# An adaLN feed-forward kernel whose opening is written out anew: w_up in quarters from ScalarE's queue, ternary weights rounded by an fp16 write, the clip inside the PSUM evacuation

## What is computed

```python
y  = einsum('bct,bcd->bdt', x, cond_weights[conditions])   # x: (64, 64, 512), a 64x64 matrix for each b
h  = act_quant(fwht(y, 512)) @ weight_quant(w_up).T        # w_up: (1024, 512)
h  = square(relu(h))
o  = act_quant(fwht(h, 1024)) @ weight_quant(w_down).T     # w_down: (512, 1024)
out = x + o
# act_quant: 8 bits with a scale for each token, from the token's largest magnitude
# weight_quant: scale = max(mean|w|, 1e-5); clip(round(w / scale), -1, 1) * scale
```

## Time and profile before

| | us |
|---|---|
| median of 3 timed runs | 296.42 |
| lowest and highest | 293.67, 298.29 |
| the profiled execution | 297.55 |
| its span, first to last instruction | 295.7 |
| TensorE busy | 254.3 (86%) |
| VectorE busy | 245.7 (83%) |
| ScalarE busy | 185.0 (63%) |
| POOL busy | 168.3 (57%) |

### The profile page before, as it was taken

One profiled execution on the slowest core, in us unless ns is written; L12 is line 12 of the kernel. 1 busy time (PEld: TensorE's weight loads), 2 busy tenths in 40 slices (PEclk: granted clock), 3 DMA queues, 4 the chain that ended last, 5 costly groups with the idle time before them and its releaser, 6 DMA issues.

```text
span 295.7 us, 6449 instructions
## 1 busy us (share of the span) xinstructions
PE 254.3 (86%) x1864; PEld 209.1 (71%) x1864; DVE 245.7 (83%) x346; ACT 185.0 (63%) x237; POOL 168.3 (57%) x200
## 2 busy tenths in 40 slices
PE   0277998979899899999899989998999999967863
PEld 0267888859688688888788878887887777635531
DVE  1168799999999988999999999999989898795451
ACT  1068677758577767675867576767676765924310
POOL 8034433595858686656595659574946548474400
PEclk9999899999999999999999999999999999995996
DMA  5585441235385946465664342433343434323262
GB/s 201 206 312 201 121 114 38 88 99 141 98 170 141 162 132 114 144 97 152 104 165 94 90 87 90 88 89 71 106 88 91 90 108 125 64 80 71 92 144 84
DMA packets 67049, 35.16 MB, mean 119 GB/s; under 512 B 57170, under 2 KB 57170, under 8 KB 67026
## 3 DMA queue, kind: packets, MB, share of 16 engines
q10 hardware_dynamic: 51200, 12.59, 24.3%
q1 hardware_dynamic: 15826, 22.29, 22.6%
HBM read 13.89 MB, written 8.39 MB: 75 GB/s over the span
## 4 chain that ended last, share of the span: by engine, by line
DVE 24%; PE 21%; POOL 19%; issue 18%; DMA 6%; ACT 6%; ACTq 2%; SPq 2%; POOLq 1%; DVEq 1%
PE u_ps L576 8%; POOL p_lo L373 8%; DVE g L699 5%; PE o_ps L586 5%; POOL x_half L340 4%; DMA uqT<-uq 4%; DVE u_max L713 3%; PE h_ps L561 3%; PE z_ps L543 3%; POOL u_deq L381 3%; DVE g L693 3%; DVE x_all L650 3%; DVE out_sb L732 2%; DVE z_max L674 2%; ACT uq L457 2%
## 5 line engine op out<-in xcount | busy, mean ns | idle before, releaser
L373 POOL TENSOR_TENSOR p_lo<-g,p_hi 128x1024 fp32r<-128x1024 f32 x32 | 82.8, 2608 | 59.3 <-ACT p_hi L452 51.8
L576 PE MATMUL u_ps<-had_r,p_hi 128*128 128x256 f32 x256 | 65.6, 293 | 11.8 <-ACT uq L457 11.5
L561 PE MATMUL h_ps<-zqT,w_upT 128*128 128x256 f16 x512 | 66.7, 273 | 2.5 <-ACT g L439 2.5
L693 DVE TENSOR_TENSOR g<-g 128x1024 f32<-128x1024 f32 x32 | 66.9, 2099 | 0.2 <-issue 0.2
L586 PE MATMUL o_ps<-w_downT,uqT 128*128 128x512 f16 x256 | 62.2, 387 | 5.1 <-DMA uqT<-uq 4.5
L576 PE MATMUL u_ps<-had_r,p_lo 128*128 128x256 f32 x256 | 63.9, 286 | 0.0
L576 PEld LDWEIGHTS u_ps<-had_r,p_hi 128*128 128x128 f32 x256 | 49.8, 195 | 16.5 <-issue 14.7
L340 POOL TENSOR_TENSOR x_half<-x_all 128x512 f32<-128x512 f32 (+1 forms) x32 | 43.5, 1361 | 21.2 <-DMA x_all<-in_x_dram 14.9
L561 PEld LDWEIGHTS h_ps<-zqT,w_upT 128*128 128x128 f16 x512 | 47.6, 98 | 10.4 <-issue 3.1
L439 ACT ACTIVATE g<-h_ps 128x512 f32<-128x512 f32 x64 | 36.5, 596 | 27.0 <-PE h_ps L561 13.0
L528 PE MATMUL y_ps<-w_diag,x_half 128*128 128x128 f32 (+1 forms) x256 | 38.5, 299 | 15.4 <-DMA w_diag<-in_L_cond_weights_dram 11.1
(11 more groups left out here) (42 smaller groups left out, 252.8 us busy)
## 6 DMA issues: line engine op xcount, KB each, us to landing
x_all<-in_x_dram SPq DMA_DIRECT2D x16, 512.0 KB, 4.2
out_dram<-out_sb SPq DMA_DIRECT2D x32, 256.0 KB, 2.0
x_all<-in_L_ffn_w_up_dram SPq DMA_DIRECT2D x2, 1024.0 KB, 7.1
x_all<-in_L_ffn_w_down_dram SPq DMA_DIRECT2D x2, 1024.0 KB, 5.9
w_diag<-in_L_cond_weights_dram SPq DMA_DIRECT2D x64, 16.0 KB, 2.4
zqT<-zq ACTq DMA_TRANSPOSE x32, 3.1
uqT<-uq ACTq DMA_TRANSPOSE x32, 3.1
x_all<-in_hadamard_dram SPq DMA_DIRECT2D x1, 256.0 KB, 3.6
```

The costliest lines, as they stand in the source:

```text
L373: nc.gpsimd.tensor_tensor(p_lo[par][:, :, i], g[par][:, :, i], p_hi[par][:, :, i].bitcast(FP32), ALU.subtract).then_inc(s_plo[k], 1)
L561: mm = nc.tensor.matmul(h_ps[u % 2][:, i, :], w_upT[:, q, f * P:(f + 1) * P], zqT[par][:, q, :], start=(q == 0), stop=(q == TC - 1))
L576: mm = nc.tensor.matmul(u_ps[:, blk * 256:(blk + 1) * 256], part[par][:, 2 * blk + i, k * P:(k + 1) * P], had_r[:, i, :], start=(i == 0 an ...
L693: nc.vector.tensor_tensor(g2[:, n, :, :], g[par][:, 0:4, :], g[par][:, 4:8, :], (ALU.add, ALU.subtract)[n]).then_inc(s_g2, 1)
```

## The change

- ScalarE's queue now issues the Hadamard matrix and w_up, the latter in four quarters, at the start of the kernel. SP's queue issues x and gathers of tiles 0 and 1 first and then w_down in four quarters.
- The memset of w_diag is in two parts: the first 4 pairs at the start, the other 28 behind the identity. Gathers of tiles 0 and 1 wait for the first part alone.
- weight_abs works on quarters, 1 and 3 on ScalarE, 0 and 2 on VectorE. weight_sum is one matmul of four columns, and VectorE adds these (one more instruction).
- weight_round replaces weight_rint: ScalarE multiplies by w_inv, with the scale in units of 2^-24, and writes fp16. The smallest step of fp16 is that unit, so the write rounds. weight_clip is gone. weight_turn transposes fp16, and weight_evac takes minimum and maximum with plus and minus one unit in place of subtracting the bias. relu multiplies by 2^24 to make up for it.
- The first five steps of each engine are no longer made from the step with once(...), but are a list, begin. In it the order differs from before, also among the stages of tiles. The drain is a list too, finish, with the same calls in the same order as before. The steps from 5 on, and the loop, are as before, with the once(...) lines gone (the weight stages that stood in step 5 are in begin).
- The waits of TensorE on the identity, the Hadamard matrix and the constants stand in the stages that use them, not ahead of everything.

The core of the diff:

```diff
-            nc.gpsimd.memset(w_diag[:, :, :], 0.0).then_inc(s_zero, 1)
+            nc.gpsimd.memset(w_diag[:, 0:2 * KP, :], 0.0).then_inc(s_zero, 1)
...
+            nc.gpsimd.memset(w_diag[:, 2 * KP:PAIRS, :], 0.0).then_inc(s_zero, 1)
...
             load_x(0, 0)
-            sp.dma_start(had_f, had).then_inc(s_had, 16)
-            load_weight(0, 0)
             gather_w(0, 0)
-            load_weight(0, 1)
             load_x(0, 1)
             gather_w(0, 1)
-            load_weight(1, 0)
-            load_weight(1, 1)
+            for u in range(4):
+                load_w_down(u)
...
-                nc.scalar.activation(part, part, ACT.Copy, scale=w_inv[:, n:n + 1], bias=RINT)\
-                    .then_inc(s_wrint[n], 1)
+                nc.scalar.activation(w_int[n][u], w_raw[n][:, u * WQ:(u + 1) * WQ], ACT.Copy,
+                                     scale=w_inv[:, n:n + 1]).then_inc(s_wrint[n], 1)
...
-                nc.vector.tensor_scalar(part, part, RINT + 1.0, RINT - 1.0, ALU.min, ALU.max)\
-                    .then_inc(s_wclip[n], 1)
...
-                nc.vector.tensor_scalar(dst, src, float(-BIAS16), None, ALU.add).then_inc(s_wT[n], 1)
+                nc.vector.tensor_scalar(dst, src, UNIT, -UNIT, ALU.min, ALU.max).then_inc(s_wT[n], 1)
...
+            act.dma_start(had_f, had).then_inc(s_had, 16)
+            for u in range(4):
+                load_w_up(u)
```

More of the change, by code:

```diff
@@ L134, in ffn_kernel @@
                  for n in range(2)]
+        w_int = [[w_raw[n][:, u * WQ:(u + 1) * WQ].bitcast(FP16)[:, 0:WQ] for u in range(4)] for n in range(2)]
         y_ps = pb("y_ps", [P, 2, TOK], FP32)
@@ L213, in value, with run_steps, at @@
             return count if isinstance(count, int) else eng.snap(count)
[L215 to L225, removed]
+        def run_steps(eng, begin, step, finish, lags):
+            def at(stage, t, *args):
+                stage(t, t // 2, t % 2, *args)
             def stages_of(half, par, s):
@@ L233, in stages_of @@
                 return run
+            begin(at)
             first = (lags + 3) // 2 * 2
-            for s in range(first):
-                step(stages_of(s // 2, s % 2, s), once_in(s))
+            for s in range(BEGIN, first):
+                step(stages_of(s // 2, s % 2, s))
             with eng.Fori(first // 2, TILES // 2) as half:
[L239 to L242, removed]
+                step(stages_of(half, 0, None))
+                step(stages_of(half, 1, None))
+            finish(at)
         @block.sync
@@ L263, in gather_w @@
                 after(sp, s_wc[par], before)
-                sp.wait_ge(s_zero, 1)
+                sp.wait_ge(s_zero, 1 if isinstance(half, int) and half == 0 else 2)
                 sp.wait_ge(s_cond, 16)
@@ L382, in u_unscale, with begin, step @@
                     .then_inc(s_udeq[k], 1)
-            def step(run, once):
+            def begin(at):
+                at(x_outer, 0, 0)
+                at(x_outer, 0, 1)
+                at(x_outer, 1, 0)
+                at(x_outer, 1, 1)
+                at(x_outer, 2, 0)
+                at(keep_z, 0)
+                at(x_outer, 3, 0)
+                at(x_outer, 2, 1)
+                at(keep_z, 1)
+                at(x_outer, 4, 0)
+                at(x_outer, 3, 1)
+                at(x_outer, 4, 1)
+            def step(run):
                 run(keep_z, 3)
@@ L464, in turn_u, with begin, step @@
                 act.dma_start(uqT[par][k][:, :, :], uq[k][:, :], transpose=True).then_inc(s_uqT[k], 16)
-            def step(run, once):
+            act.dma_start(had_f, had).then_inc(s_had, 16)
+            for u in range(4):
+                load_w_up(u)
+            def begin(at):
+                weight_abs(0, 1)
+                at(y_high, 0, 0)
+                weight_abs(0, 3)
+                weight_round(0, 0)
+                at(y_high, 0, 1)
+                weight_round(0, 1)
+                weight_round(0, 2)
+                weight_round(0, 3)
+                at(y_high, 1, 0)
+                at(quant_z, 0, 0)
+                weight_abs(1, 1)
+                weight_abs(1, 3)
+                at(y_high, 1, 1)
+                at(quant_z, 0, 1)
+                weight_round(1, 0)
+                weight_round(1, 1)
+                at(turn_z, 0, 0)
+                at(quant_z, 1, 0)
+                at(y_high, 2, 0)
+                at(turn_z, 0, 1)
+                weight_round(1, 2)
+                at(relu, 0, 1)
+                at(turn_z, 1, 0)
+                at(relu, 0, 0)
+                at(y_high, 2, 1)
+                at(quant_z, 1, 1)
+                at(relu, 0, 2)
+                at(square, 0, 0)
+                at(y_high, 3, 0)
+                at(relu, 0, 3)
+                at(square, 0, 1)
+                at(quant_z, 2, 0)
+                at(turn_z, 1, 1)
+                weight_round(1, 3)
+                at(y_high, 3, 1)
+                at(quant_z, 2, 1)
+                at(turn_z, 2, 0)
+                at(relu, 1, 1)
+                at(relu, 1, 0)
+                at(y_high, 4, 0)
+                at(square, 1, 0)
+                at(relu, 1, 3)
+                at(turn_z, 2, 1)
+                at(quant_z, 3, 0)
+                at(p_high, 0, 0)
+                at(y_high, 4, 1)
+                at(relu, 1, 2)
+                at(square, 1, 1)
+                at(quant_z, 3, 1)
+                at(p_high, 0, 1)
+                at(turn_z, 3, 0)
+            def step(run):
                 run(y_high, 0, 0)
[L468 to L471, removed]
                 run(relu, 3, 0)
@@ L749, in step @@
+            def step(run):
+                run(g_inner, 5, 0)
                 run(y_low, 1, 1)
@@ L785, in hadamard @@
+            run_steps(dve, begin, step, finish, 7)
 def hadamard(n):
```

419 lines of the change are left out of this document (332 added, 87 removed).

## The result

The changed kernel takes 305.52 us in the median (304.39 to 305.97), the kernel before 295.62 in the runs of the same comparison. The ratio is 1.035, interval 1.028 to 1.042: slower, by about 10 us, and above the top of the range of the prediction.

What follows compares the result with a forecast made beforehand. The opening was taken as bound by VectorE with TensorE close behind. Order +1.3 and clock +1.3 gave 2.6 us: 300.2 on the profiled execution, 299.0 on the median; range 291.5 to 302.5.

Steps and rivals of the forecast that it cites:

- The first 18 us: Kernel start: first project moves from 11.12 to about 10.0, and w_inv is ready at about 15.3, 3.4 us earlier.
- From there to the first up: From w_inv: had_z(0,0) 4.3 us earlier; quant_z(1,0) releases the transpose at 29.3, landing at 31.8; 2.0 us of lead left.
- The mechanism of the ups: Ups waiting for transposes make TensorE stand 2.1 us ahead of up(0,1) and 3.6 us ahead of up(1,1).
- The clock: Opening, behind TensorE's standstills: one stretch at the lower clock level counted, +1.3 us, range 0 to 3.4.
- The base: Trace of the kernel before, 297.55 us: TensorE waited 1.54 us, then ran at the lower clock from 28.3 to 31.6.
- The clips: VectorE in the opening: eight clips, 9.2 us, go, but can't give back their whole length with TensorE close behind.
- The sums: Whole kernel: +1.3 by the order and +1.3 by the clock, 2.6 us slower, 299.0 on the median.
- The third rival: Opening: low clock behind both standstills, +3.4 instead of +1.3, +1.5 until had_z(0,1), order 1.3: 302.6 us; chance 0.15.
- Its other term: Third rival, start of the opening: TensorE reaches the full clock level only after had_z(0,1), +1.5 us.

Runs made afterwards that it cites:

- the gathers first: New parts in the old order of stages, with w_up's last two quarters issued only after the first gathers landed: 293.44 us, ratio 0.993.
- The two lists: Changed kernel with two ScalarE entries moved (300.03 us), or with had_z(1,1), project(3,1), had_z(2,1) moved ahead of ups on TensorE (299.84 us); together 299.07 us.
- the parts in the old order: Changed kernel with every new part, but the first six steps' stages in the order of the kernel before: 294.32 us, ratio 0.999.
- clock held up: Changed kernel with unused matmuls added, 36 ahead of up(0,1) and 31 ahead of up(1,1): 302.06 us, ratio 1.030.
- Rounding alone: Kernel before with only the fp16 rounding, fp16 transposes and minimum and maximum in the evacuation, no clips: 292.70 us, ratio 0.991.
- both orders with p_high early: Changed kernel with the ScalarE and TensorE moves, and p_high(0,1) right behind p_high(0,0) on ScalarE: 297.53 us, ratio 1.002.
- turn_z(0,0) early: Changed kernel with one ScalarE entry moved, turn_z(0,0) ahead of y_high(1,1): 301.75 us, ratio 1.022.
- the DMA part alone: Kernel before with only the new DMA queues, the quarters of w_up and w_down, and the two-part memset: 293.91 us, ratio 0.998.
- ScalarE's list: Changed kernel with turn_z(0,1) moved ahead of quant_z(1,0) and turn_z(1,1) ahead of quant_z(2,0): 300.03 us, ratio 1.020.
- both orders: Changed kernel with two turn_z entries moved earlier on ScalarE, and had_z(1,1), project(3,1), had_z(2,1) ahead of ups on TensorE: 299.07 us, ratio 1.016.

## Why the prediction was wrong

The forecast was a loss of 2.6 us against the median, and 10 were lost. The step that failed is the wait ahead of up(0,1), in which quant_z(1,0) was costed by its scale alone; beside it the clock term was too small. Against the same trace of before, the second p_low was to end at 63.7 (62.4 and 1.3 for the clock) and ended at 69.5. Step by step:

- **The first 18 us**: wrong by 1.5. The gathers were issued at 3.00, 2.2 us earlier than before and earlier than I took, but the first project came at 11.46, not at 10.0, because the gathers had all of w_up beside them: those of tile 0 took 5.1 us to landing in the median. I had bounded the start of the issue, with a gain between 0 and 2.5, and left the landing as it was; the first project came 0.3 later than before. The kernel with the gathers first, with 9.14, shows that this was the cause. w_inv came at 16.5 instead of 15.3.
- **From there to the first up**: the step that failed. I had the transpose of zq(0,1) released at 29.3 by "quant_z(1,0)", once its scale was there. quant_z has a second wait, on the transpose that last read its buffer, and the new order issues that transpose at 28.46 because it stands behind weight_round(1,0). up(0,1) came at 35.21, not at 31.8: 1.2 of it inherited (the scale at 30.45), 1.8 this wait (to 32.23), and 0.4 a transpose that took 2.8 and not 2.4. The same second wait struck again at quant_z(3,0), at 60.97, whose buffer's transpose took 5.3 us to land; p_high(0,0) stands behind it and came at 61.55. I costed quant_z by the wait for its scale alone and left out the one that frees its buffer. Taking this wait away at quant_z(1,0), by one moved entry, gave back 3.8 us of the 10.
- **The mechanism of the ups**: right, including where it would show, ahead of up(0,1) and up(1,1), with 4.53 and 3.96 us of standing against 2.1 and 3.6. up(1,1) came at 49.32 against 44.1. The two lists can't be parted (5.5, 5.7, both 6.5 us).
- **The clock**: the term was mis-sized. I counted 1.3 us for one stretch of 3.3. The changed kernel was at the low level for most of 32 to 36, for all of 36 to 40, and again around 52; holding it up is worth 4.5 us at the first p_low, and 3.5 in the median with the doubt said above. The sum held the smaller value of a range that ended at 3.4.
- **The base**: TensorE's low stretch at 28 us in the trace of before was taken for a part of that kernel. It is there in two of its three traces, behind a wait that a long clip had made 1.1 us longer. Against an execution without it the true cost of the changed opening is 9.3 us (first p_low at 53.43 and at 62.68). By single traces this is a gain of 2.5 by the parts in the old order (50.92), a loss of 7.3 by the order's standstills (58.20, clock held up), and one of 4.5 by the clock. The first of these three comes from an execution 1.8 us below its kernel's median, and that median is only 0.8 below the kernel before.
- **The clips**: right that VectorE's 9.2 us wouldn't come back whole. Rounding alone gave 2.4.
- **The sums** agree with their terms to 0.3 us, but for the end of had_z(3,1), 56.2, which the terms before it put at 55.5. Neither matters beside a miss of 5.8 us at the hand-over.

The third rival had the right decision point: the low clock did follow both standstills, at once at up(0,1), and behind up(1,1), which still took 1.03 us, at project(3,1), 1.78 us long. It had 302.6 where 305.5 was measured. Its other term, the full level only after had_z(0,1), +1.5, did not occur. In the changed kernel had_z(0,1) begins with the row that had_z(1,1) has at the full level in the earlier trace rows; in had_z(0,0), at 19.29, the same matmul took 0.55:

```profile
24.40 0.36 PE L689 MATMUL z_ps<-had_r,y_hi 128*128 128x256 f32 x1 [0.86 <-DVE y_lo L872]
```

So what brought that rival near the measured time is in part luck: without this term it stands at 301.1. Its 0.15 was too little for a case that the low clock behind the trace's own 1.54 us wait spoke for. The Trainium skill ("TensorE: Matmul & The Clock Gate", HAM oscillation) describes a matmul kernel that waits 3 to 5 us for data at each of its steps and begins each next step at half rate. The waits of 4.53 and 3.96 us agree with it. Shorter waits, which that section does not describe, went both ways here: the clock was low behind 1.54, 2.39 and 2.83 us (the kernel before, both orders with p_high early, turn_z(0,0) early) and stayed at 1.00 behind 1.29, 2.10 and 2.46 (the DMA part alone, ScalarE's list, both orders). With the buffer's wait of 1.8 us and the larger clock term of 3.4 in the sum, the forecast would have been 303 by estimate, still 2.6 short of the measured median.

## What to carry to other kernels

In a hand-made order, list for each entry all of its waits, the one that frees its output buffer too: a transpose by DMA of 128x512 fp16 holds the buffer that it reads for 2.4 to 5.3 us here, so it should be issued as soon as its input is there, and never behind an entry that waits for something younger. A standstill of TensorE of some 4 us had to be counted twice here, once as itself and once as the low clock behind it; behind one of 1.5 to 3 us the low clock is a chance to be priced, not a certainty. And take a trace of before twice, or hold its time against the median, before its stalls are taken for properties of the kernel.

## What the runs showed of the hardware

- More bulk in flight slows small DMAs: the four 16 KB gathers of tile 0 took 5.1 us to landing in the median with 2 MB of w_up issued beside them from another queue (5.2 in the old order), and 3.0 with the second half of w_up held back. With the first half of w_up ahead of them in their own queue, as in the kernel before, the first three took 2.9. The share of the DMA engines was near 1 until 11 us in the changed kernel, and fell to 0.36 at 8 us in the kernel before. Moving w_up's 2 MB to a second queue, with the split memset, gained nothing (ratio 0.998).
- Extra matmuls whose results nobody uses kept the granted clock at 1.00 through two waits of some 4 us, and brought the first p_low from 62.68 to 58.20; the median of four executions was 3.5 us lower.
- Behind waits of TensorE of 1.3 to 2.8 us the granted clock was low in some traces and at 1.00 in others, even in two kernels whose lists are the same up to that wait (2.39 us: 0.73 and 0.85 in the windows 32 to 36 and 36 to 40; 2.46 us: 1.00 in both).
- A clip of 128x1024 fp32 on VectorE took 1.70 and 1.75 us in two traces and 0.69 in a third, a difference of 1.0 us in the opening of one and the same kernel, of which the low clock behind it made more.
- A minimum and maximum from PSUM with fp16 in and out cost 0.67 to 0.68 us for 128x1024, the same as the subtraction from int16 before.
